# An earlier place for phi in the first loads, and a new order of the lists in the first dispatch of a fused attention and soft-mixture kernel

## The reference

```
def _L0_attn_ref(x, norm_w, norm_b, qkv_w, qkv_b, proj_w, proj_b):
    h = _layernorm(x, norm_w, norm_b)
    q, k, v = split(einsum('btc,oc->bto', h, qkv_w) + qkv_b)
    attn = einsum('btc,bsc->bts', q, k) / sqrt(C)          # no softmax
    o = einsum('bts,bsc->btc', attn, v)
    return x + einsum('btc,oc->bto', o, proj_w) + proj_b
def _L0_ffn_ref(x, phi, W, b):
    logits = einsum('bmd,dnp->bmnp', x, phi)
    dispatch = softmax(logits, axis=0)                     # over the two batches
    combine = softmax(logits.reshape(b, m, n * p), axis=-1)
    slots = einsum('bmd,bmnp->bnpd', x, dispatch)
    y = einsum('bnpd,nde->bnpe', slots, W) + b
    return einsum('bnpd,bmnp->bmd', y, combine)
x = x + _layernorm(_L0_attn_ref(_layernorm(x), ...))
x = x + _layernorm(_L0_ffn_ref(_layernorm(x), ...))
```

## Time and profile before

| | us |
|---|---|
| median of 3 runs | 641.18 |
| the profiled execution, its own time | 641.88 |
| its span, first to last instruction | 640.1 |
| TensorE busy | 628.2 |
| VectorE busy | 447.9 |
| ScalarE busy | 359.0 |
| GpSimd busy | 230.2 |

### The profile page before, as it was taken

How to read it: one execution, slowest core, us unless ns; L and a number is a source line. 1 busy time by engine, 2 the same in 40 slices (tenths; PEclk the granted TensorE clock), 3 DMA queues, 4 the chain that set the end, 5 groups by cost and what they waited for, 6 DMA issues and landing times.

```text
span 640.1 us, 15341 instructions
## 1 busy us (share of the span) xinstructions
PE 628.2 (98%) x5351; PEld 395.4 (62%) x5351; DVE 447.9 (70%) x857; ACT 359.0 (56%) x694; POOL 230.2 (36%) x410
## 2 busy tenths in 40 slices
PE   8999999999999999999999999999999999999996
PEld 8898644545444444444444457777777777777776
DVE  5978888835244453446344399999888888888886
ACT  5666776843233232224444356777777777777764
POOL 5375896820000000000000001555555555555554
PEclk9999999999999999999999999999999999999999
DMA  8920032325766666666555531222222222222201
GB/s 266 402 77 1 1 67 50 67 60 156 201 176 176 177 193 185 173 178 203 135 136 186 159 104 67 91 90 90 90 90 90 90 90 90 90 90 90 90 16 34
DMA packets 78485, 77.07 MB, mean 120 GB/s; under 512 B 6386, under 2 KB 74995, under 8 KB 76147
## 3 DMA queue, kind: packets, MB, share of 16 engines
q1 hardware_dynamic: 76112, 74.48, 38.4%
q10 hardware_dynamic: 2338, 2.16, 1.0%
HBM read 51.71 MB, written 23.07 MB: 117 GB/s over the span
## 4 chain that ended last, share of the span: by engine, by line
PE 79%; DVE 8%; POOL 5%; issue 3%; DMA 2%; ACT 2%; SPq 1%; DVEq 0%; POOLq 0%; ACTq 0%
PE psL L1568 24%; PE psM L1555 11%; PE psL L1687 11%; PE psM L1705 7%; PE psM L1709 7%; PE psM L1706 7%; PE psM L1585 3%; POOL small L492 2%; DMA r_xn<-in_proj_wT 2%; PE psL L1773 1%; PE psL L1453 1%; PE psM L1511 1%; DVE phs L1091 1%; DVE small L1286 1%; DVE r_xn L1305 1%
## 5 line engine op out<-in xcount | busy, mean ns | idle before, releaser
L1568 PE MATMUL psL<-r,r_xn 128*128 128x512 f16 x768 | 176.3, 379 | 0.8 <-DVE r L1112 0.8
L1568 PEld LDWEIGHTS psL<-r,r_xn 128*128 128x128 f16 x768 | 73.4, 98 | 91.0 <-issue 7.0
L762 ACT ACTIVATE r<-psM,small 128x512 f32<-128x512 f32 x64 | 43.7, 682 | 96.3 <-PE psM L1555 95.5
L1555 PE MATMUL psM<-phs,xx 128*128 128x512 f16 (+1 forms) x384 | 93.2, 379 | 0.9 <-DVE xx L1146 0.9
L580 POOL MEMSET r_xn<- 128x8 f16 x2 | 0.3, 137 | 234.2 <-PE psL L1568 234.2
L1110 DVE TENSOR_SCALAR r<-r 128x512 f16<-128x512 f32 x64 | 28.5, 445 | 71.8 <-ACT r L762 71.8
L1687 PE MATMUL psL<-phs,r 128*32 128x512 f16 x1344 | 75.1, 379 | 0.0
L1555 PEld LDWEIGHTS psM<-phs,xx 128*128 128x128 f16 x384 | 37.3, 98 | 45.9 <-DVE xx L1146 1.4
L875 ACT ACTIVATE r<-psL,small 128x512 f32<-128x512 f32 x60 | 41.9, 776 | 37.7 <-DVE small L1313 37.4
L492 POOL TENSOR_TENSOR small<-small,epst 128x2 f32<-128x2 f32 (+3 forms) x75 | 59.8, 797 | 6.2
L1687 PEld LDWEIGHTS psL<-phs,r 128*32 128x32 f16 x1344 | 34.6, 97 | 36.5 <-issue 3.0
(11 more groups left out here) (200 smaller groups left out, 1260.8 us busy)
## 6 DMA issues: line engine op xcount, KB each, us to landing
r<-in_ffn_w SPq DMA_DIRECT2D x23, 1024.0 KB, 5.8
logit_difference<-r SPq DMA_DIRECT2D x256, 64.0 KB, 1.9
xx<-logit_difference SPq DMA_DIRECT2D x16, 1024.0 KB, 4.8
out<-r SPq DMA_DIRECT2D x32, 128.0 KB, 1.7
xres<-in_x SPq DMA_DIRECT2D x7, 512.0 KB, 11.4
r<-in_phi SPq DMA_DIRECT2D x1, 2048.0 KB, 19.3
expert_bias<-r ACTq DMA_DIRECT2D x1, 2048.0 KB, 21.6
r<-expert_bias SPq DMA_DIRECT2D x16, 128.0 KB, 5.5
```

The costliest lines, as they stand in the source:

```text
L1555: ins = mm(bk[j % 2][:, :].rearrange("p (q m) -> p q m", q=EP), xxT[:, 1, j, hx, k, :], phw[:, hp, k, :, bass.ds(nb, 1), :].rearrange("p q ...
L1568: ins = mm(psL[:, i * 512:(i + 1) * 512], x3n[:, b, j, hx, k * P:(k + 1) * P], thl[:, j % 2, hs, :], start=(j == 0 and hx + hs == 0), stop ...
```

## The change

- X_GROUPS has 11 groups where there were 9: tiles 0 and 1 of batch 0 singly, then 2 + 2 + 2, and 4 from there on. Tile 1 is loaded by ScalarE's queue.
- The loads' order becomes x of batch 0, w_raw, wbc, bbc, qbc, x group 7, wpT, x group 8, phi, x groups 9 and 10, expert weights. wpT gets a semaphore of its own.
- VectorE takes the maximum of phi ahead of the statistics of the last two groups, and `bias_row(0)` moves between the two halves of phi. TensorE's `phi_turn` goes ahead of `A_step(0)`, and `phi_broadcast` two tiles earlier.
- GpSimd makes `residual_terms(0)` ahead of batch 1's terms; `ident16` and `fold_weights` move from there to the end of its dispatch list. SyncE waits for `ident16` before it loads over the unit matrix, and VectorE for the masks before it uses them.
- In the dispatch lists, ScalarE's tanh(0,0), xd_hi(1), tanh(0,3) and xd_hi(2) come earlier, VectorE's residual(1,2) later, and TensorE's turn_xd(3) and turn_xd(4) later.

```diff
-            for g in range(NG + 1):
-                load_x(g)
+            for g in range(NG):
+                if g != 1:
+                    load_x(g)
             sp.dma_start(w_raw, ...).then_inc(par_loaded, 16)
...
-            sp.dma_start(wpT, ...).then_inc(par_loaded, 16)
-            for g in range(NG + 1, XG + 1):
-                load_x(g)
+            load_x(NG)
+            sp.dma_start(wpT, ...).then_inc(wpT_loaded, 16)
+            load_x(NG + 1)
             sp.dma_start(phf, phi_v).then_inc(phi_loaded, 16)
+            load_x(NG + 2)
+            load_x(NG + 3)
...
+            sp.wait_ge(ident16_ready, 1)
             for w in range(2):
                 sp.dma_start(byx[:, w], b_v[NT - 2 + w]).then_inc(b23_loaded, 16)
...
-            pool.wait_ge(r0_ready, 2)
-            nc.gpsimd.tensor_scalar(ident16, ...)      # to the end of the dispatch list
-            fold_weights()
...
         def _(act):
+            act.dma_start(xres[:, 0, 1:2, :], x_v[:, 0, 1:2, :]).then_inc(x_loaded[1], 16)
...
-            x3_float(0, 1); xd_hi(0); x3_hi(0, 1); y_squares(1, 4); x3_float(1, 1); y_squares(1, 5)
-            act.wait_ge(phi_split, 1); tanh(0, 0); x3_float(0, 2); d_copy(0, 0); xd_hi(1); tanh(0, 1)
+            x3_float(0, 1); xd_hi(0); x3_hi(0, 1); y_squares(1, 4); x3_float(1, 1)
+            act.wait_ge(phi_split, 1); tanh(0, 0); y_squares(1, 5); xd_hi(1); x3_float(0, 2); d_copy(0, 0); tanh(0, 1)
...
-            bias_row(0)
+            stats(NG + 2)
             dve.wait_ge(phi_row, 1)
             V.tensor_reduce(gm[0:1, 0:1], bk[0][0:1, 0:P], AX_X, ALU.max).then_inc(phi_top, 1)
+            stats(NG + 3)
...
                 if t == NJ + 5:
+                    phi_turn()
                     A_step(0)
                 if t == NJ + 6:
-                    phi_turn()
-                if t == NJ + 8:
                     phi_broadcast()
...
-            d_first(3); turn_xd(2); slots_first(2); d_first(4); slots_first(3); turn_xd(3)
-            d_first(5); slots_first(4); d_first(6); slots_first(5); h_pair(1, 6); d_first(7)
-            turn_xd(4); slots_first(6); h_pair(1, 7); d_first(8); slots_first(7); turn_xd(5)
+            d_first(3); turn_xd(2); slots_first(2); d_first(4); slots_first(3); d_first(5)
+            turn_xd(3); slots_first(4); d_first(6); slots_first(5); h_pair(1, 6); d_first(7)
+            slots_first(6); turn_xd(4); h_pair(1, 7); d_first(8); slots_first(7); turn_xd(5)
```

More of the change, by code:

```diff
@@ L104, in build @@
     GJ = 4
-    XG = B * NJ // GJ
-    NG = NJ // GJ
+    X_GROUPS = [(0, 0, 1), (0, 1, 1), (0, 2, 2), (0, 4, 2), (0, 6, 2)] + [
+        (b, j, GJ) for b in range(B) for j in range(0, NJ, GJ) if b or j >= 2 * GJ]
+    XG = len(X_GROUPS)
+    NG = XG - NJ // GJ
     assert (B, K, TB) == (2, 2, 4)
@@ L254, in build @@
         bk = [psM[:, i * 512:(i + 1) * 512] for i in range(4)]
-        par_loaded, rows_loaded = sem("par_loaded"), sem("rows_loaded")
-        x_loaded = [sem(f"x_loaded{g}") for g in range(XG + 1)]
+        par_loaded, rows_loaded, wpT_loaded = sem("par_loaded"), sem("rows_loaded"), sem("wpT_loaded")
+        x_loaded = [sem(f"x_loaded{g}") for g in range(XG)]
         phi_loaded = sem("phi_loaded")
@@ L316, in build @@
         y_lots = [(1, 0), (1, 1), (0, 0), (0, 1), (1, 2), (0, 2), (1, 3), (0, 3)]
-        N_PAR = 5
-        X_GROUPS = [(0, 0, 2), (0, 2, 2)] + [(b, j, GJ) for b in range(B) for j in range(0, NJ, GJ) if b + j]
+        N_PAR = 4
         GROUP_OF = {(b, j + i): g for g, (b, j, n) in enumerate(X_GROUPS) for i in range(n)}
@@ L359, in _ @@
             sp.dma_start(qbc, qkv_b).then_inc(par_loaded, 16)
-            sp.dma_start(wpT, proj_wT.rearrange("(k p) e -> p k e", p=P)).then_inc(par_loaded, 16)
-            for g in range(NG + 1, XG + 1):
-                load_x(g)
+            load_x(NG)
+            sp.dma_start(wpT, proj_wT.rearrange("(k p) e -> p k e", p=P)).then_inc(wpT_loaded, 16)
+            load_x(NG + 1)
             sp.dma_start(phf, phi_v).then_inc(phi_loaded, 16)
+            load_x(NG + 2)
+            load_x(NG + 3)
             for w in range(2):
@@ L504, in x_terms @@
                 own.add(nc.gpsimd.tensor_scalar(e2, mvx[:, b, tn, 1], 1.0 + EPS, EPS * EPS, ALU.mult, ALU.add))
+                own.add(nc.gpsimd.tensor_scalar(nm, mvx[:, b, tn, 0], -1.0, 0.0, ALU.mult, ALU.add))
                 own.wait()
                 own.add(rsqrt(r1[:, b, tn], e2))
-                own.add(nc.gpsimd.tensor_scalar(nm, mvx[:, b, tn, 0], -1.0, 0.0, ALU.mult, ALU.add))
                 own.wait()
@@ L521, in residual_terms @@
                 nc.gpsimd.tensor_tensor(n0[:, b], nm, r0[:, b], ALU.mult).then_inc(r0_ready, 1)
-            for g in range(XG + 1):
+            for g in range(NG):
                 x_terms(g)
             residual_terms(0)
+            for g in range(NG, XG):
+                x_terms(g)
             residual_terms(1)
-            pool.wait_ge(r0_ready, 2)
-            nc.gpsimd.tensor_scalar(ident16, ident, 1.0, 0.0, ALU.mult, ALU.add).then_inc(ident16_ready, 1)
-            fold_weights()
             def y_terms(b, p):
@@ L573, in _ @@
             y_terms(1, 7); x3_terms(0, 7); x3_lo(1, 6); x3_lo(0, 7); x3_terms(1, 7); x3_lo(1, 7)
+            pool.wait_ge(r0_ready, 2)
+            nc.gpsimd.tensor_scalar(ident16, ident, 1.0, 0.0, ALU.mult, ALU.add).then_inc(ident16_ready, 1)
+            fold_weights()
             pool.wait_ge(ry_ready, B * NJ // 2)
@@ L801, in _ @@
             y_squares(1, 2); y_squares(1, 3); y_squares(0, 4); x3_float(1, 0); x3_hi(1, 0); y_squares(0, 5)
-            x3_float(0, 1); xd_hi(0); x3_hi(0, 1); y_squares(1, 4); x3_float(1, 1); y_squares(1, 5)
-            act.wait_ge(phi_split, 1); tanh(0, 0); x3_float(0, 2); d_copy(0, 0); xd_hi(1); tanh(0, 1)
+            x3_float(0, 1); xd_hi(0); x3_hi(0, 1); y_squares(1, 4); x3_float(1, 1)
+            act.wait_ge(phi_split, 1); tanh(0, 0); y_squares(1, 5); xd_hi(1); x3_float(0, 2); d_copy(0, 0); tanh(0, 1)
             x3_hi(1, 1); d_copy(0, 1); x3_hi(0, 2); y_squares(0, 6); tanh(0, 2); x3_float(1, 2)
-            d_copy(0, 2); x3_hi(1, 2); x3_float(0, 3); tanh(0, 3); xd_hi(2); d_copy(0, 3)
+            d_copy(0, 2); x3_hi(1, 2); tanh(0, 3); xd_hi(2); x3_float(0, 3); d_copy(0, 3)
             x3_hi(0, 3); x3_float(1, 3); x3_hi(1, 3); tanh(0, 4); d_copy(0, 4); xd_hi(3)
@@ L1039, in primed_weights @@
                 V.tensor_tensor(w_aug[:, :, C - 1], bcol, qbc, ALU.add).then_inc(wprime_ready, 1)
[L1041 to L1045, removed]
+            for g in range(NG):
+                stats(g)
             proj_bias()
             weight_scale()
-            stats(5)
+            stats(NG)
             own.add(V.tensor_reduce(bmx, bT.rearrange("p k n -> p (k n)"), AX_X, ALU.max, apply_absolute_value=True))
@@ L1087, in _ @@
                     own.add(V.tensor_scalar(phs[:, 0, k, c].rearrange("p (t c) -> p t c", c=Q), src, sg[:, 0:1], None, ALU.mult))
+            bias_row(0)
             own.wait()
@@ L1154, in _ @@
             add_x(0, 5); xd_diff(0); stats_x2(1, 1); add_x(1, 4); stats_x2(0, 2); xd_lo(0)
-            add_x(1, 5); residual(1, 2); add_x(0, 6); xd_diff(1); split(0, 0); stats_x2(1, 2)
+            add_x(1, 5); add_x(0, 6); xd_diff(1); split(0, 0); residual(1, 2); stats_x2(1, 2)
             xd_lo(1); split(0, 1); stats_x2(0, 3); residual(1, 3); split(0, 2); xd_diff(2)
```

6 lines of the change are left out of this document (3 added, 3 removed).

## The result

The change made the kernel slower: 643.09 us (median of 7 runs, 642.37 to 645.36) against 641.18, a ratio of 1.0036 with a 95% interval of 1.0024 to 1.0047. The forecast was 639.0, in a range of 636.8 to 641.1. The profiled execution has a span of 641.3 and a time of 643.21; before it was 640.1 and 641.88.

The account below looks back on a forecast made before the run. TensorE, 98% busy, loses time in the front and the dispatch, where GpSimd's chain paces it from 65.8. Front 1.1; chain lead 1.5 plus 0.6 gives 2.1, taken as 2.2: 641.18 - 2.2 = 639.0, range 636.8 to 641.1.

Parts of the forecast that it names:

- the front: Everything before the dispatch: TensorE enters the dispatch 0.46 + 0.3 + 0.36 = 1.1 us sooner, and GpSimd's chain too.
- First groups: TensorE's tiles 3 and 4: tile 4 waits for a group of two instead of four; 0.46 us won, bounds 0 and 0.46.
- wpT: Tile 16 in the front: wpT off the common semaphore frees VectorE sooner; 0.3 us won, bounds 0 and 0.9.
- the lock: VectorE two-SBUF-input and SBUF-reading GpSimd instructions exclude each other; a difference takes 1.64 under low halves, 0.69 away.
- phi: phi's earlier landing: 0 by itself, but bias_row(1) no longer late, so the wait behind h_pair(0,3) goes: 0.36 us.
- ident16 and fold_weights: About 4 us of GpSimd moved to its list's end near 135; idle in both places, so 0.
- Dispatch lists: Waits at turn_xd(1), d_first(4) and turn_xd(4) go; lead 1.5 us at slots_first(4), 2.7 if no halves are stretched.
- The tail rule: End of the dispatch: TensorE's lead cannot exceed the chain's lead plus 0.6, so 1.5 + 0.6 = 2.1 us.
- Rival 3: Dispatch: VectorE's halves newly meet GpSimd's low halves, about 0.95 each, four of them 3.8; time 642.8; chance 0.10 with late phi.

Follow-up runs that it names:

- a7: The changed kernel with residual_terms(0) behind all groups' terms again, batch 0's first loads in groups of pairs, and the old dispatch lists: 639.53 us, ratio 0.9974.
- a3: The changed kernel with residual_terms(0) behind all groups' terms again and batch 0 loaded in groups of 2, 2, 2, 2, 4, 4 tiles; new lists kept: 640.63 us.
- a1: The changed kernel with only residual_terms(0) put back behind the terms of all groups on GpSimd: 641.37 us, ratio 0.9997 to the kernel before.
- a4: The changed kernel with VectorE's wide two-input subtract of the weights left out of the computation: 641.61 us, ratio 1.0009 to the kernel before.
- a5: a3 with phi put back as before (load, maximum, turn, spread and bias row): 640.76 us, ratio 0.9996 to the kernel before.
- a2: The changed kernel with all three engines' old dispatch lists, its front kept: 642.90 us, ratio 1.0027 to the kernel before.
- d2: a3, new lists kept, with VectorE's stats_x2(0,4) ahead of xd_diff(3) and split(0,4): 640.77 us, ratio 0.9996 to the kernel before.
- c4: a7, old lists kept, with VectorE's stats_x2(0,4) ahead of xd_diff(3) and split(0,4): 638.72 us, ratio 0.9962 to the kernel before.
- d1: a3 with the first block's second split halves reading one input instead of two, tangent's low half left out: 638.12 us, ratio 0.9954 to the kernel before.
- b2: The kernel before with one edit, residual_terms(0) on GpSimd ahead of batch 1's terms: 640.73 us, ratio 0.9993.

## Why the prediction was wrong

Three steps failed: the moves on GpSimd were priced at 0 with residual_terms(0) left out, the two more rounds of terms were put where GpSimd waits, and the dispatch lists were priced by the waits that they remove. By the medians the parts add up like this. The change's front with old lists, pairs and the residual terms put back (a7) is 1.5 below the kernel before (639.53 against 641.04), where the text gave the front 1.1. The new lists lose 1.1 (a3), the single tiles 0.7 (a1) and the place of the residual terms 1.7 (the change as it is).

- **First groups**, forecast 0.46 won: measured 0.19 lost at tile 5. The term failed. Its text named two more rounds of about 1.5 for GpSimd and put them where GpSimd waits; but before the change its one wait behind the first terms was 0.78, at 8.81, ahead of tile 4's. The rounds stand in a row ahead of tile 2, whose terms ended 1.1 us later than before. The load of one tile also came no sooner: VectorE's first statistics started at 3.90 (before 3.84). With pairs (a3) tile 5 starts 4.37 behind tile 0 instead of 4.84, so the forecast of 0.46 holds.
- **wpT**, forecast 0.3 won at tile 16: 1.6 lost. The step that failed is the sentence on ident16 and fold_weights, and what it leaves out: of the moves on GpSimd it counts those two and not residual_terms(0), named in the list of the change and 3.9 us long. VectorE was as early as forecast. a1 gives 1.7 for the place, a4 1.5 for the lock behind it, and the two overlap.
- **phi**, forecast 0 by itself and 0.36 through the bias row. The maximum started at 26.12 and phs at 40.74 in the changed kernel, since TensorE had come late. The wait behind h_pair(0,3) did go. a5 has it back with 0.26, so the mechanism was right and the size near; the time can't tell it (0.1 by the medians).
- **ident16 and fold_weights**, forecast 0: they ran at 136.7 to 139.9 and nobody waited.
- **Dispatch lists**, forecast 1.1 won: 1.1 lost (a3 against a7). The waits that the text names went, stayed and came as it has them, but it has none at slots_first(9). Two things failed. First, the text let the lock stretch VectorE's instructions only; it stretched GpSimd's too, and the new lists add 1.4 to a chain that the text had treated as a fixed row of durations (8.56 in a2 to 9.98 in the changed kernel). Second, it booked the 0.81 at turn_xd(4) as won, while the later turn holds ScalarE and, through it, GpSimd (d2). The rows that it started from hide the first: they are of an execution with a stretch of 9.77 already. In that pair of profiles x3_terms(1,2) ends at 84.52 before and 86.03 after, 1.5 later instead of 1.1 sooner, and 1.3 of it is late at the chain's trigger already (65.80 and 67.12).
- **The tail rule**, TensorE's lead is the chain's plus 0.6: from slots_first(4) to the token sums all kernels but c4 and d1 take 39.98 to 40.05. That the end hangs on slots_first(4) was right. What fills the stretch behind it differs: with the old lists one wait at turn_xd(4), with TensorE's new one the later waits that turn_xd(4) causes. That both come to 1.0 is chance, as far as these runs show. The text adds 1.5 and 0.6 to 2.1 and then takes 2.2.
- **Rival 3**, slower by halves under low halves, had 0.10 and comes nearest by its time (642.8), and that is luck. Its meetings of VectorE's halves with low halves lie in the dispatch; most of the loss was made in the front, and in the dispatch it was GpSimd that was held.

The sum by spans: 1.8 later at the first h_pair, 0.6 won back by the token sums, 1.2 in the span. The medians say 1.9. Most of the 0.7 between them is that the profiled execution of the kernel before lies 0.7 above its median and that of the changed kernel only 0.1.

## What to carry to other kernels

When an engine's work comes earlier, list everything in front of its consumer on every engine, with the length of each piece: a hole that hid 4 us (GpSimd from 14.2 to 20.5) can be closed by the change itself. Where VectorE and GpSimd hold each other up, the length of a short instruction is no constant; find in a trace which instructions keep their length beside the other engine's long ones, and put those there (here the statistics, but not the first half of a split, though both read one input). And give a list's move its price by what it does to the chain, not by the wait that it removes: whoever waits for the moved instruction has its own list standing still.

## What the hardware showed

- A GpSimd instruction of 0.20 took 1.68 beside a VectorE subtract with two SBUF inputs, and 0.20 without it (a4).
- VectorE's statistics kept their 0.75 for two under GpSimd's low halves (c4). A difference went from 0.69 to 1.61 there (the changed kernel), and the one-input first half of a split from 0.42 to 1.38 (c4).
- With unchanged lists, GpSimd's stretch between two low halves was 9.77 before and 8.57 in b2, whose front alone differs, in one execution each. In the first, VectorE's two-input half of a split started at 81.15, just ahead of GpSimd's root at 81.25, which took 1.15; in the second it started at 80.91, just behind the root at 80.68, which took 0.74. So such a row of instructions can move by 1.2 us with the phase of the engines.
